# The first pass of a graph network: aggregation placed inside the other stream's layer, and stores issued by ScalarE

## Chip, cores, metric

One NeuronCore of a Trainium2 chip. The metric is the device time of one execution in microseconds (us), the slowest core's; with one core it is that core's. Three runs of the kernel before gave 2013.59, 2016.44 and 2018.27 us, median 2016.44.

## What is computed

Four layers over x of 128 graphs x 64 nodes x 256 features with one 64 x 64 adjacency matrix; each layer adds a graph network's output to x and normalises. Layer 0, whose first half is the subject here, is

```python
A_norm = A + eye(n)
deg = sum(A_norm, axis=0) + sum(A_norm, axis=1) - diagonal(A_norm)
A_hat = A_norm * rsqrt(deg)[:, None] * rsqrt(deg)[None, :]
agg = einsum('nm,bmd->bnd', A_hat, x)
h = relu(batchnorm(agg.reshape(-1, d) @ W1.T + b1, g1, be1))     # 256 -> 512
out = batchnorm(h @ W2.T + b2, g2, be2)                          # 512 -> 256
x = layernorm(x + out)
```

Layer 1 is a Chebyshev convolution with the largest eigenvalue of the matrix, attention and a feed-forward part; layer 2 two graph convolutions and LSTMs over windows; layer 3 a graph attention. The batch norms take their mean and variance over all 8192 tokens, so layer 0 needs three passes over the tokens.

## The kernel before

All weights stay in SBUF, each split into a high and a low f16 part (`w_hi`, `w_lo`), so that a product takes three f16 matmuls (L454 to L456: high x high, high x low, low x high). Tokens come in 16 tiles of 512 (8 graphs); tile (r, s) belongs to round r of 8 and stream s of 2. Each stream has its own buffers and its own 4 PSUM banks `ps[s]` of 512 f32 columns.

Three blocks follow one another. Block 1 (L562 to L879), the subject, computes for every tile h = agg @ W1.T + b1, its statistics, and stores h to DRAM (`h_scratch`). Block 2 (L895 to L1088) reads h back, applies the batch norm and relu and multiplies by W2. Block 3 is the rest of the network, some 1770 us, whose order of work per engine is written out by hand in `ORDER`.

Block 1, per engine. The engines run their own lists in order and meet only at semaphores.

- TensorE (PE), L747 to L768. `aggregate(s, n)` (L724): 64 matmuls of 64 x 64 in f32 (`quarters`, L468) into banks 0 and 1 of `ps[s]`, after waiting for the tile of x and for the four reads of the stream's banks. `hidden(s, n, ms)` (L734): 6 matmuls of 128 x 512 for each of four output parts m; the banks are 2, 3, 0, 1 for stream 0 and 2, 0, 1, 2 for stream 1. `square(j, which)` (L717): the squarings of a 64 x 64 matrix for the eigenvalue, one or two small f32 matmuls that depend on DVE. A round is aggregate(0), aggregate(1), then for each stream hidden m 0 and 1, square, hidden m 2 and 3, square.
- ScalarE (ACT), L699 to L708. `agg_high` (L678) casts the aggregate to f16 (L680); `unit_high` (L672) casts one unit of 1408 weight columns (L675); `hid_bias` (L682) moves the four parts from PSUM to `hid[s]` with the bias (L687), after waiting until the store of the stream's last tile has landed and its statistics are taken. A round is agg_high(0), agg_high(1), then for each stream unit_high and hid_bias of four.
- VectorE (DVE), L843 to L860. `agg_low` (L830) takes the low part of the aggregate (L832); `unit_low` (L777) that of the weights (L780); `hid_stat` (L835) the statistics of `hid` of the round before (L838); `square` (L818) the normalisation, copy and trace (L821 to L827).
- SyncE (SP), L591 to L609, issues all DMAs: `load_x` (L586), 512 KB, after the tile's aggregate; `load_unit` (L582), 704 KB, after DVE has used the unit before; `store` (L577), 1024 KB, after the tile's four biases. A round is load_x(0), load_x(1), then for each stream load_unit and store.

The weights are read in 16 units in the course of the block, two a round; W1 is in unit 0.

Of the kernel before, what the change touches and what calls it, by code (L numbers as in the profile page):

```python
# [8 lines left out]
ALU = mybir.AluOpType  # L9
# [3 lines left out]
P = 128  # L13
# [7 lines left out]
HT = HID // P  # L21
# [354 lines left out]
def build(nc, x, adj, adj_t, wpack, w3t, cols, rows, out):  # L376
    ctx = ExitStack()
    with ctx:
# [120 lines left out]
        with ExitStack() as pctx:  # L499
# [48 lines left out]
            spare = ps[1][:, BANKS - 1, :]  # L548
            SQ, TR, LAM, WA = spare[0:NODES, 0:NODES], spare[:, 64:65], spare[:, 66:68], spare[:, 72:72 + 2 * KT]

            GCN, SUMS = (ps[0][:, BANKS - 1, j * P:(j + 1) * P] for j in range(2))
            def aggregated(s):
                return ps[s][:, 0:2, :].rearrange('p c (j n) -> p j c n', n=NODES)

# [7 lines left out]
            @block.sync  # L562
            def _(sp):
                sp.wait_ge(zeroed, 2)
                for b in range(2):
                    d = slice(b * NODES, (b + 1) * NODES)
                    sp.dma_start(a_bd[d, d], adj).then_inc(adj_in, 16)
                    sp.dma_start(at_bd[d, d], adj_t).then_inc(adj_in, 16)
                for s in range(STREAMS):
                    sp.dma_start(xa[s][:, :, :], x_tiles[1, s]).then_inc(x_in[s], 16)  # L570
                sp.dma_start(stage[0], wpack[:, 0:UNIT]).then_inc(w_in[0], 16)
                sp.dma_start(col[:, :], cols).then_inc(vec_in, 16)
                sp.dma_start(stage[1], wpack[:, UNIT:2 * UNIT]).then_inc(w_in[1], 16)
                sp.dma_start(w3t_sb[:, 0:KT, :], w3t).then_inc(vec_in, 16)
                sp.dma_start(row[:, :, :], rows.partition_broadcast(P)).then_inc(row_in, 16)

                def store(s, n):  # L577
                    sp.wait_ge(hid_out[s], n * HT + 1)
                    sp.dma_start(h_tiles[bass.ds(n, 1), s].rearrange("o p m n -> (o p) m n"), hid[s])\
                        .then_inc(hid_stored[s], 16)  # L580

                def load_unit(r, b):  # L582
                    sp.wait_ge(unit_lo, r * STAGES + b - (STAGES - 1))
                    sp.dma_start(stage[b], wpack[:, bass.ds(r * (STAGES * UNIT) + b * UNIT, UNIT)]).then_inc(w_in[b], 16)

                def load_x(s, r, tile):  # L586
                    sp.wait_ge(agg_ps[s], r)
                    sp.dma_start(xa[s][:, :, :], x_tiles[bass.ds(tile, 1), s].rearrange("o p b d -> (o p) b d"))\
                        .then_inc(x_in[s], 16)

                for b in range(STAGES):  # L591
                    load_unit(1, b)
                with sp.Fori(1, ROUNDS - 1) as r:
                    for s in range(STREAMS):
                        load_x(s, r, r + 1)
                    for s in range(STREAMS):
                        load_unit(r + 1, s)
                        store(s, r)

                for s in range(STREAMS):  # L600
                    load_x(s, ROUNDS - 1, 0)
                for s in range(STREAMS):
                    store(s, ROUNDS - 1)
                for s in range(STREAMS):
                    sp.wait_ge(unit_lo, UNITS)
                    sp.wait_ge(hid_stored[s], 17)
                    sp.dma_start(first_hid[s], h_tiles[1, s]).then_inc(h_in[1][s], 16)
                for s in range(STREAMS):
                    sp.wait_ge(hid_stored[s], 16 * (ROUNDS - 1) + 1)  # L609
# [56 lines left out]
            @block.scalar  # L666
            def _(act):
                act.wait_ge(ident_ok, 5)
                for s in range(STREAMS):
                    nc.scalar.activation(small[:, 40 + s:41 + s], ident[:, 0:1], ACT.Copy).then_inc(hid_out[s], 1)  # L670

                def unit_high(r, b):  # L672

                    act.wait_ge(w_in[b], r * 16 + 16)
                    nc.scalar.activation(w_hi[:, bass.ds(r * (STAGES * UNIT) + b * UNIT, UNIT)], stage[b], ACT.Copy,  # L675
                                         scale=WSCALE).then_inc(unit_hi, 1)

                def agg_high(s, n):  # L678
                    act.wait_ge(agg_ps[s], n)
                    nc.scalar.copy(by_batch(hl_a[s][:, 0, :, :]), aggregated(s)).then_inc(agg_hi[s], 1)  # L680

                def hid_bias(s, n):  # L682
                    act.wait_ge(hid_stored[s], n * 16 - 15)
                    act.wait_ge(hid_stats[s], n)
                    for m in range(HT):
                        act.wait_ge(hid_ps[s], n * HT - (HT - 1 - m))
                        nc.scalar.activation(hid[s][:, m, :], ps[s][:, hid_bank[s][m], :], ACT.Identity,  # L687
                                             bias=vec("b1", m), scale=UNSCALE).then_inc(hid_out[s], 1)

                unit_high(0, 0)  # L690
                act.wait_ge(step, 7)
                for j in range(HALF):
                    part = slice(j * P, (j + 1) * P)
                    nc.scalar.copy(sums[0:1, part], SUMS[0:1, :])
                    nc.scalar.copy(sums[64:65, part], SUMS[64:65, :])
                    nc.scalar.copy(sums[32:33, part], SUMS[32:33, :]).then_inc(rows_ok, 1)
                unit_high(0, 1)
                act.wait_ge(vec_in, 32)
                with act.Fori(0, ROUNDS - 1) as r:  # L699
                    for s in range(STREAMS):  # L700
                        agg_high(s, r + 1)
                    for s in range(STREAMS):
                        unit_high(r + 1, s)
                        hid_bias(s, r + 1)
                for s in range(STREAMS):
                    agg_high(s, ROUNDS)
                for s in range(STREAMS):
                    hid_bias(s, ROUNDS)  # L708

            @block.tensor  # L710
            def _(pe):
# [5 lines left out]
                def square(j, which):  # L717
                    pe.wait_ge(sq_ready, j * 3 + 2 + which)
                    pe.sem_inc(begun, 1)
                    if which == 0:  # L720
                        nc.tensor.matmul(TR, ones[0:NODES, :], tr_part, start=True, stop=True)
                    nc.tensor.matmul(SQ, powr, powr, start=True, stop=True).then_inc(sq_ps, 1)
# [21 lines left out]
                        mm.then_inc(hid_ps[s], 1)  # L744

                pe.wait_ge(step, 7)
                with pe.Fori(0, ROUNDS - 1) as r:  # L747
                    for s in range(STREAMS):
                        aggregate(s, r + 1)
                    for s in range(STREAMS):  # L750
                        hidden(s, r + 1, range(HT // 2))
                        square(r * STREAMS + s, 0)
                        hidden(s, r + 1, range(HT // 2, HT))
                        square(r * STREAMS + s, 1)
                for s in range(STREAMS):
                    aggregate(s, ROUNDS)
                hidden(0, ROUNDS, range(HT))
                pe.wait_ge(vec_in, 32)
                pe.wait_ge(sq_ready, 3 * (SQUARINGS // 2) + 3)
                nc.tensor.matmul(LAM, ones[0:NODES, :], lam_part, start=True, stop=True)  # L760
# [10 lines left out]
            def _(dve):  # L771
# [5 lines left out]
                def unit_low(r, b):  # L777
# [2 lines left out]
                    nc.vector.scalar_tensor_tensor(w_lo[:, part], stage[b], WSCALE, w_hi[:, part], ALU.mult,  # L780
                                                   ALU.subtract).then_inc(unit_lo, 1)

                dve.wait_ge(adj_in, 64)
                dve.wait_ge(ident_ok, 5)

# [12 lines left out]
                nc.vector.tensor_scalar(scaled, junk_full, dinv, None, ALU.mult).then_inc(step, 1)  # L798
                dve.wait_ge(gcn_ps, 1)
                nc.vector.tensor_scalar(gcn_t[:, :], GCN, dinv, None, ALU.mult).then_inc(step, 1)  # L800
                unit_low(0, 0)

                nc.vector.tensor_tensor(sym, a_bd[0:NODES, 0:NODES], at_bd[0:NODES, 0:NODES], ALU.add).then_inc(step, 1)
# [23 lines left out]
                        nc.vector.tensor_tensor_reduce(junk, powr, powr, 1.0, 0.0, ALU.mult, ALU.add, tr_part)\  # L827
                            .then_inc(sq_ready, 1)

                def agg_low(s, n):  # L830
                    dve.wait_ge(agg_hi[s], n)
                    nc.vector.tensor_tensor(by_batch(hl_a[s][:, 1, :, :]), aggregated(s), by_batch(hl_a[s][:, 0, :, :]), ALU.subtract)\  # L832
                        .then_inc(agg_lo[s], 1)

                def hid_stat(s, r, ms):  # L835
                    for m in ms:
                        dve.wait_ge(hid_out[s], r * HT + m + 2)
# [4 lines left out]

                with dve.Fori(0, ROUNDS - 1) as r:  # L843
                    for s in range(STREAMS):
                        agg_low(s, r + 1)
                    for s in range(STREAMS):
                        unit_low(r + 1, s)
                        hid_stat(s, r, range(HT // 2))
                        square(r * STREAMS + s, 0)
                        hid_stat(s, r, range(HT // 2, HT))  # L850
                        square(r * STREAMS + s, 1)
                for s in range(STREAMS):
                    agg_low(s, ROUNDS)
                dve.wait_ge(sq_ready, 3 * (SQUARINGS // 2) + 2)
                nc.vector.tensor_tensor_reduce(junk, sym, powr, 1.0, 0.0, ALU.mult, ALU.add, lam_part[:, 0:1])\
                    .then_inc(pow_ok, 1)
                dve.wait_ge(pow_ok, 2)
                nc.vector.tensor_tensor_reduce(junk, ident[0:NODES, 0:NODES], powr, 1.0, 0.0, ALU.mult, ALU.add,
                                               lam_part[:, 1:2]).then_inc(sq_ready, 1)
                hid_stat(0, ROUNDS - 1, range(HT))  # L860


                dve.wait_ge(hid_stats[0], ROUNDS + 1)
# [1281 lines left out]
```

## Time and profile before

| | us |
|---|---|
| median of three runs | 2016.44 |
| the profiled execution | 2013.94 |
| its span, first to last instruction | 2012.1 |
| block 1, until PE's last hidden product ends | about 143.5 |
| waits of PE for DVE L832 in block 1 | 16.0 |

The busy times of the page are sums over the whole span. A timeline row gives start, duration, engine, line and operation, with the idle time of the engine before it in brackets. PEld is PE's loading of weights, which overlaps its matmuls; a matmul of 512 columns has a duration of 0.38 us there, though they start 0.22 us apart, since they are pipelined. "DMA share" is the mean busy share of 16 DMA engines, as the tool gives it; it goes slightly above 1 in short windows.

### The profile page before, as it was taken

Reading aid. Unit: us, or ns where it says so; the run is one execution under the profiler, and the core shown is the slowest. Engines: PE = TensorE matmul, PEld = TensorE weight load, DVE = VectorE, ACT = ScalarE, POOL = GpSimd, SP = SyncE. Lnnn points to the kernel's source line nnn. Section 1 sums busy time; section 2 is a strip of 40 time slices with the busy share of each in tenths; the row PEclk is TensorE's granted clock in tenths of the full one; section 3 lists DMA queues with packets and bytes.
Section 4 is the critical chain, followed back from the end, with each engine's and each line's share of the span. In section 5 each row is a group of like instructions: output and inputs, shape, how many; then the busy total and the mean of one; then the engine's idle time right before and its main releaser. Section 6 shows DMA issues by size and latency. Waiting matters only on the chain.

```text
span 2012.1 us, 85711 instructions
## 1 busy us (share of the span) xinstructions
PE 1944.8 (97%) x37031; PEld 1730.6 (86%) x37031; DVE 1718.2 (85%) x4795; ACT 1443.6 (72%) x4475; POOL 187.8 (9%) x258
## 2 busy tenths in 40 slices
PE   6899989999999999999999999999999999999997
PEld 3444469999999999999999999999999999999996
DVE  6779897888888988898889888898889888988866
ACT  5657537777777777767777777777777777777777
POOL 2000010110101010101001110101010101111000
PEclk9999999999999999999999999999999999999999
DMA  7857400000100001000100010000000010000000
GB/s 281 290 196 253 175 2 23 14 13 4 44 3 24 3 3 45 13 13 3 44 14 13 4 44 4 23 3 14 34 13 13 3 45 13 13 3 13 3 3 23
DMA packets 36822, 87.79 MB, mean 44 GB/s; under 512 B 2416, under 2 KB 26992, under 8 KB 32752
## 3 DMA queue, kind: packets, MB, share of 16 engines
q1 hardware_dynamic: 36464, 82.56, 11.8%
q8 instruction: 280, 4.59, 1.0%
q14 instruction: 78, 0.64, 0.1%
HBM read 52.15 MB, written 30.41 MB: 41 GB/s over the span
## 4 chain that ended last, share of the span: by engine, by line
PE 78%; ACT 5%; DVE 4%; issue 1%; POOL 0%; ACTq 0%; DVEq 0%
PE ps L1539 18%; PE ps L1568 11%; PE ps L1548 9%; PE ps L1353 8%; PE ps L1387 7%; PE ps L1575 5%; PE ps L1363 4%; PE ps L1395 3%; PE ps L468 2%; PE ps L1330 2%; ACT pool_mem L1726 2%; PE ps L1320 1%; PE ps L1627 1%; PE ps L1595 1%; PE ps L1441 1%; DVE stats L1849 1%
## 5 line engine op out<-in xcount | busy, mean ns | idle before, releaser
L1726 ACT ACTIVATE pool_mem<-ps,lstm_b 128x64 f32<-128x64 f32 (+2 forms) x2496 | 606.2, 364 | 147.0 <-PE ps L1575 102.6
L1539 PE MATMUL ps<-hl_a,w_hi 128*128 128x64 f16 (+1 forms) x3584 | 361.3, 205 | 1.8 <-DVE hl_a L2005 0.9
L1539 PE MATMUL ps<-hl_a,w_lo 128*128 128x64 f16 (+1 forms) x3584 | 360.8, 205 | 0.0
L1818 POOL TENSOR_TENSOR rstd<-mv,nhalf 128x2 f32<-128x2 f32 x224 | 174.1, 779 | 1592.3 <-DVE mv L1853 1592.3
L1539 PEld LDWEIGHTS ps<-hl_a,w_hi 128*128 128x128 f16 x3584 | 284.4, 97 | 6.3 <-DVE hl_a L2005 1.2
L1539 PEld LDWEIGHTS ps<-hl_a,w_lo 128*128 128x128 f16 x3584 | 283.0, 97 | 2.8
L1568 PE MATMUL ps<-pool_mem,w_hi 128*128 128x64 f16 (+2 forms) x3072 | 273.6, 200 | 0.0
L1568 PE MATMUL ps<-pool_mem,w_lo 128*128 128x64 f16 (+2 forms) x3072 | 273.5, 199 | 0.0
L1548 PE MATMUL ps<-hl_a,w_hi 128*128 128x64 f16 (+1 forms) x3584 | 233.5, 205 | 0.2 <-issue 0.2
L1568 PEld LDWEIGHTS ps<-pool_mem,w_hi 128*128 128x128 f16 x3072 | 228.9, 98 | 2.9
L1568 PEld LDWEIGHTS ps<-pool_mem,w_lo 128*128 128x128 f16 x3072 | 227.7, 98 | 0.7
L1548 PEld LDWEIGHTS ps<-hl_a,w_hi 128*128 128x128 f16 x3584 | 177.4, 97 | 0.9 <-issue 0.3
L1575 PE MATMUL ps<-pool_mem,w_hi 128*128 128x64 f16 (+2 forms) x3072 | 175.4, 200 | 0.0
L1849 DVE BATCH_NORM_STATS2 stats<-t 128x6 f32<-128x256 f32 x448 | 168.2, 417 | 5.5
L1735 ACT ACTIVATE pool_mem<-pool_mem 128x256 f32<-128x256 f32 (+2 forms) x352 | 129.2, 379 | 53.2 <-DVE pool_mem L1989 28.7
L1983 DVE SCALAR_TENSOR_TENSOR pool_mem<-pool_mem 128x256 f32<-128x256 f32 (+2 forms) x352 | 118.8, 340 | 38.7 <-ACT pool_mem L1726 36.4
L1387 PE MATMUL ps<-hl_b,w_hi 128*128 128x256 f16 x640 | 150.3, 273 | 0.4 <-DVE hl_b L1898 0.2
L1387 PE MATMUL ps<-hl_b,w_lo 128*128 128x256 f16 x640 | 150.2, 273 | 0.0
L2002 DVE SCALAR_TENSOR_TENSOR pool_mem<-pool_mem 128x256 f32<-128x256 f32 (+2 forms) x352 | 123.9, 356 | 28.9 <-ACT pool_mem L1735 27.8
L1575 PEld LDWEIGHTS ps<-pool_mem,w_hi 128*128 128x128 f16 x3072 | 135.9, 98 | 0.0
L1539 PE MATMUL ps<-hl_b,w_hi 128*128 128x84 f16 x1408 | 130.4, 201 | 0.5
L1539 PE MATMUL ps<-hl_b,w_lo 128*128 128x84 f16 x1408 | 130.5, 200 | 0.0
(253 smaller groups left out, 4768.8 us busy)
## 6 DMA issues: line engine op xcount, KB each, us to landing
xa<-in_x SPq DMA_DIRECT2D x32, 512.0 KB, 5.4
h_scratch<-pool_mem SPq DMA_DIRECT2D x14, 1024.0 KB, 4.4
pool_mem<-h_scratch SPq DMA_DIRECT2D x14, 1024.0 KB, 6.8
pool_mem<-in_wpack SPq DMA_DIRECT2D x16, 704.0 KB, 4.2
out<-xb SPq DMA_DIRECT2D x16, 512.0 KB, 3.4
o_scratch<-act_in SPq DMA_DIRECT2D x14, 512.0 KB, 3.2
act_in<-o_scratch SPq DMA_DIRECT2D x14, 512.0 KB, 5.0
row<-in_rows SPq DMA_DIRECT2D x1, 1408.0 KB, 11.7
```

The costliest lines, as they stand in the source:

```text
L1353: nc.tensor.matmul(tok(s, bank)[:, b, :], hi, w[part], start=k == 0 and b == 0 and part == 0, stop=False, skip_group_check=True)
L1387: nc.tensor.matmul(out[:, j, :], w[part], hi[:, k, :], start=j == 0 and k == 0 and part == 0, stop=False, skip_group_check=True)
L1539: nc.tensor.matmul(o, wk[part], toks[0][:, k], start=(g, m) == gms[0] and k == 0 and part == 0, stop=False, skip_group_check=True)
L1548: mm = nc.tensor.matmul(o, weight(f"wih{p}", k, (g * KT + m) * P, P)[0], toks[1][:, k], start=False, stop=step == 0 and (g, m) == gms[-1] ...
L1568: nc.tensor.matmul(gate_place(s, h, g, m, w), wk[part], hi[:, k * w:(k + 1) * w], start=False, stop=False, skip_group_check=True)
L1575: mm = nc.tensor.matmul(gate_place(s, h, g, m, w), weight(f"whh{p}", k, (g * KT + m) * P, P)[0], lo[:, k * w:(k + 1) * w], start=False, st ...
L1726: op = nc.scalar.activation(gates[s][h][:, g, m * w:(m + 1) * w], gate_place(s, h, g, m, w), ACT.Tanh, bias=lstm_b[:, bias:bias + 1], scal ...
L1735: nc.scalar.activation(cell_t[s][h][:, 0:KT * w], cell_c[s][h][:, 0:KT * w], ACT.Tanh, scale=0.5)\
L1818: nc.gpsimd.tensor_tensor(rstd[s][:, blocks(h)], mv[s][:, blocks(h), 1], nhalf[:, 0:HALF], ALU.pow)\
L1849: nc.vector.bn_stats(stats[s][:, b, 0:6], t[s][:, b, :]).then_inc(ln_step.of(s, h), 1)
L1983: nc.vector.scalar_tensor_tensor(cc if first else g[GATE_I], g[GATE_I], 1.0, g[GATE_G], ALU.add, ALU.mult).then_inc(cell_dve.of(s, h), 1)
L2002: nc.vector.scalar_tensor_tensor(to, o, 1.0, th, ALU.add, ALU.mult).then_inc(cell_dve.of(s, h), 1)
```

## The change

In block 1 the aggregate of the other stream goes between the two halves of a stream's `hidden` on PE, and the cast, the subtraction and the loads of ACT, DVE and SP are put in the matching order; aggregate(0, 1) is done ahead of the loop. The stores of h leave SP's list and are issued by ACT. `SUMS` moves to another bank. Cut to what matters:

```diff
-            GCN, SUMS = (ps[0][:, BANKS - 1, j * P:(j + 1) * P] for j in range(2))
+            GCN = ps[0][:, BANKS - 1, 0:P]
+            SUMS = ps[1][:, 2, 0:P]
 SP
+                load_x(0, 1, 2)
                 for b in range(STAGES):
                     load_unit(1, b)
-                with sp.Fori(1, ROUNDS - 1) as r:
-                    for s in range(STREAMS):
-                        load_x(s, r, r + 1)
+                load_x(1, 1, 2)
+                with sp.Fori(1, ROUNDS - 2) as r:
                     for s in range(STREAMS):
                         load_unit(r + 1, s)
-                        store(s, r)
-
+                        load_x(s, r + 1, r + 2)
                 for s in range(STREAMS):
+                    load_unit(ROUNDS - 1, s)
                     load_x(s, ROUNDS - 1, 0)
-                for s in range(STREAMS):
-                    store(s, ROUNDS - 1)
 ACT
-                def hid_bias(s, n):
-                    act.wait_ge(hid_stored[s], n * 16 - 15)
-                    act.wait_ge(hid_stats[s], n)
-                    for m in range(HT):
+                def hid_bias(s, n, ms):
+                    if 0 in ms:
+                        act.wait_ge(hid_stored[s], n * 16 - 15)
+                        act.wait_ge(hid_stats[s], n)
+                    for m in ms:
...
+                def store(s, n):
+                    act.wait_ge(hid_out[s], n * HT + 1)
+                    nc.scalar.dma_start(h_tiles[bass.ds(n, 1), s].rearrange("o p m n -> (o p) m n"), hid[s])\
+                        .then_inc(hid_stored[s], 16)
+
+                agg_high(0, 1)
                 unit_high(0, 0)
...
                 with act.Fori(0, ROUNDS - 1) as r:
-                    for s in range(STREAMS):
-                        agg_high(s, r + 1)
-                    for s in range(STREAMS):
-                        unit_high(r + 1, s)
-                        hid_bias(s, r + 1)
-                for s in range(STREAMS):
-                    agg_high(s, ROUNDS)
-                for s in range(STREAMS):
-                    hid_bias(s, ROUNDS)
+                    hid_bias(0, r + 1, range(HT // 2))
+                    agg_high(1, r + 1)
+                    unit_high(r + 1, 0)
+                    hid_bias(0, r + 1, range(HT // 2, HT))
+                    store(0, r + 1)
+                    hid_bias(1, r + 1, range(HT // 2))
+                    agg_high(0, r + 2)
+                    unit_high(r + 1, 1)
+                    hid_bias(1, r + 1, range(HT // 2, HT))
+                    store(1, r + 1)
+                hid_bias(0, ROUNDS, range(HT // 2))
+                agg_high(1, ROUNDS)
+                hid_bias(0, ROUNDS, range(HT // 2, HT))
+                hid_bias(1, ROUNDS, range(HT))
 PE
                 pe.wait_ge(step, 7)
+                aggregate(0, 1)
+                pe.wait_ge(unit_lo, 1)
                 with pe.Fori(0, ROUNDS - 1) as r:
-                    for s in range(STREAMS):
-                        aggregate(s, r + 1)
                     for s in range(STREAMS):
                         hidden(s, r + 1, range(HT // 2))
                         square(r * STREAMS + s, 0)
+                        aggregate(1 - s, r + 1 + s)
                         hidden(s, r + 1, range(HT // 2, HT))
                         square(r * STREAMS + s, 1)
-                for s in range(STREAMS):
-                    aggregate(s, ROUNDS)
-                hidden(0, ROUNDS, range(HT))
+                hidden(0, ROUNDS, range(HT // 2))
+                aggregate(1, ROUNDS)
+                hidden(0, ROUNDS, range(HT // 2, HT))
 DVE
                 nc.vector.tensor_scalar(gcn_t[:, :], GCN, dinv, None, ALU.mult).then_inc(step, 1)
+                agg_low(0, 1)
                 unit_low(0, 0)
...
                 with dve.Fori(0, ROUNDS - 1) as r:
                     for s in range(STREAMS):
-                        agg_low(s, r + 1)
-                    for s in range(STREAMS):
+                        hid_stat(s, r, range(1))
+                        square(r * STREAMS + s, 0)
+                        hid_stat(s, r, range(1, HT // 2))
+                        agg_low(1 - s, r + 1 + s)
                         unit_low(r + 1, s)
-                        hid_stat(s, r, range(HT // 2))
-                        square(r * STREAMS + s, 0)
+                        square(r * STREAMS + s, 1)
                         hid_stat(s, r, range(HT // 2, HT))
-                        square(r * STREAMS + s, 1)
-                for s in range(STREAMS):
-                    agg_low(s, ROUNDS)
...
-                hid_stat(0, ROUNDS - 1, range(HT))
+                hid_stat(0, ROUNDS - 1, range(HT // 2))
+                agg_low(1, ROUNDS)
+                hid_stat(0, ROUNDS - 1, range(HT // 2, HT))
```

## Rows read from the trace of the kernel before

**Rows 1.** The page's first part: busy time, share and instructions of each engine.
```profile
PE 1944.8 (97%) x37031; PEld 1730.6 (86%) x37031; DVE 1718.2 (85%) x4795; ACT 1443.6 (72%) x4475; POOL 187.8 (9%) x258
```

**Rows 2.** Waits, 0 to 145 us: engine, line, releaser, total us, times, longest.
```profile
PE ps L454 <- DVE hl_a L832: 16.0, 8, 5.6
ACT w_hi L675 <- DMA pool_mem<-in_wpack: 11.0, 2, 8.1
```

**Rows 3.** Timeline of one round, 60 to 80 us, around the aggregates.
```profile
63.95 1.99 PEld L468 LDWEIGHTS ps<-gcn_t,xa 64*64 64x64 f32 x128
...
65.23 1.95 ACT L680 CAST hl_a<-ps 128x1024 f16<-128x1024 f32 x2 [0.55 <-PE ps L468]
65.43 0.20 DVE L825 COPY x<-ps 64x64 f32<-64x64 f32 x1
...
65.81 0.08 DVE L827 DVE_READ_ACCUMULATOR2_ANT setup<- 64x1 f32 x1
66.27 2.35 DVE L832 TENSOR_TENSOR hl_a<-ps,hl_a 128x1024 f16<-128x1024 f32 x2 [0.39 <-ACT hl_a L680]
...
67.55 0.39 PE L454 MATMUL ps<-hl_a,w_hi 128*128 128x512 f16 x1 [1.48 <-DVE hl_a L832]
...
69.06 0.69 ACT L687 ACTIVATE pool_mem<-ps,col 128x512 f32<-128x512 f32 x1 [0.61 <-PE ps L456]
```

**Rows 4.** Timeline, 110 to 150 us: the same start in the last round.
```profile
130.89 0.39 PE L454 MATMUL ps<-hl_a,w_hi 128*128 128x512 f16 x1 [1.48 <-DVE hl_a L832]
```

**Rows 5.** Windows: length, busy us and instructions of each engine, granted clock, DMA share, GB/s.
```profile
63.90:79.80 15.90, 14.42 (x190) 7.63 (x190) 12.28 (x23) 9.87 (x12) 0.00 (x0) 1.00 0.83 289
...
70.00:72.00 2.00, 2.00 (x12) 1.08 (x11) 1.61 (x5) 0.69 (x1) 0.00 (x0) 1.00 1.16 390
```

**Rows 6.** Timeline, stream 1's half of that round.
```profile
73.76 0.39 PE L454 MATMUL ps<-hl_a,w_hi 128*128 128x512 f16 x1
...
76.45 0.29 PEld L721 LDWEIGHTS ps<-setup,x 64*128 64x128 f32 x2 [0.42 <-issue]
...
76.56 0.69 ACT L687 ACTIVATE pool_mem<-ps,col 128x512 f32<-128x512 f32 x1 [0.42 <-PE ps L456]
76.76 0.19 PEld L722 LDWEIGHTS ps<-x 64*64 64x64 f32 x2
...
77.02 0.39 PE L454 MATMUL ps<-hl_a,w_hi 128*128 128x512 f16 x1
```

**Rows 7.** Timeline, 57 to 62 us: a weight unit on ACT and DVE.
```profile
58.37 1.37 ACT L675 ACTIVATE w_hi<-pool_mem 128x1408 f32 x1
...
59.89 1.63 DVE L780 SCALAR_TENSOR_TENSOR w_lo<-pool_mem,w_hi 128x1408 f32 x1 [0.21 <-ACT w_hi L675]
```

**Rows 8.** Timeline, 0 to 34 us: the start of block 1.
```profile
9.29 3.53 PEld L468 LDWEIGHTS ps<-gcn_t,xa 64*64 64x64 f32 x128 [1.10 <-issue]
...
11.20 1.38 ACT L675 ACTIVATE w_hi<-pool_mem 128x1408 f16<-128x1408 f32 x1 [8.13 <-DMA pool_mem<-in_wpack]
...
14.26 3.43 SPq L584 DMA_DIRECT2D pool_mem<-in_wpack  x2
...
18.65 0.61 PE L454 MATMUL ps<-hl_a,w_hi 128*128 128x512 f16 x1 [5.64 <-DVE hl_a L832]
...
20.27 1.38 ACT L675 ACTIVATE w_hi<-pool_mem 128x1408 f32 x1 [2.84 <-DMA pool_mem<-in_wpack]
...
21.19 0.54 PE L454 MATMUL ps<-hl_a,w_hi 128*128 128x512 f16 x1
```

**Rows 9.** SP's wait, 15 to 145 us; issues (ns min/median/max) of x and stores; stores' landing.
```profile
SPq L579 <- ACT pool_mem L687: 49.0, 14, 7.2
...
L588 SPq DMA_DIRECT2D xa<-in_x x14: 383/396/1257, 18.0 to 113.7; - x14
...
L579 SPq DMA_DIRECT2D h_scratch<-pool_mem x14: 355/362/382, 27.0 to 128.0; - x14
...
DMA to landing us min/median/max: 3.9/4.4/5.1
```

More of the change, by code:

```diff
@@ L575, in _ @@
                 sp.dma_start(row[:, :, :], rows.partition_broadcast(P)).then_inc(row_in, 16)
[L577 to L580, printed above, removed]
                 def load_unit(r, b):
@@ L781, in unit_low, with agg_low @@
                                                    ALU.subtract).then_inc(unit_lo, 1)
+                def agg_low(s, n):
+                    dve.wait_ge(agg_hi[s], n)
+                    nc.vector.tensor_tensor(by_batch(hl_a[s][:, 1, :, :]), aggregated(s), by_batch(hl_a[s][:, 0, :, :]), ALU.subtract)\
+                        .then_inc(agg_lo[s], 1)
                 dve.wait_ge(adj_in, 64)
@@ L828, in square @@
                             .then_inc(sq_ready, 1)
[L830 to L833, printed above, removed]
                 def hid_stat(s, r, ms):
```

## The prediction

> **What bounds the kernel now.** The page comes first: TensorE (PE) is busy for 97% of the span [rows 1], so time comes off almost only where PE stands still or does other work. The change touches the first block alone, so next come its waits [rows 2]. The reader is to see one large wait of PE: 8 times, once per round, it stood before a `hidden` for DVE's `agg_low` (L832), 16.0 us in all, 5.6 the first time. Third, a round at close hand [rows 3]: both aggregates run back to back (128 weight loads, 1.99 us from 63.95), ScalarE (ACT) casts both (from 65.23), DVE subtracts (from 66.27), and PE starts `hidden(0)` at 67.55, having stood still for 1.48 us. Fourth, the same hidden start 4 rounds later is at 130.89 [rows 4], so a round is (130.89 - 67.55)/4 = 15.83 us. In such a round DVE is busy for 12.28 us, ACT for 9.87, and the DMA engines 0.83 of the time at 289 GB/s [rows 5]. Three resources thus stand not far behind PE.
>
> **Part 1, aggregation inside the other stream's layer, steady rounds.** No matmul, cast or subtraction is added or removed; they move. Half a round, in PE's own time from its first hidden matmul, is read from stream 1's half, which no aggregate cuts today [rows 6]: start 73.76, the first squaring's loads at 76.45 (2.69), the second pair of products at 77.02 (3.26). The other half's 67.55 to 73.76 is 6.21. An aggregate costs 1.99/2 = 1.0 us of loads [rows 3]. So a half becomes 6.2 + 1.0 = 7.2 and a round 14.4, if nothing waits: 15.83 - 14.4 = **1.4 saved in each of 7 rounds, 9.9 us**. The switch back from small f32 loads to a hidden matmul inside a layer is not in the trace; after a squaring it takes 0.07 (0.19 of loads from 76.76, then 77.02), after an aggregate it may take from nothing to 0.28 (from the end of a first aggregate's loads, 63.95 + 1.0, to its cast at 65.23, the row nearest to a drained array). I take the 0.07, small f32 loads too, and keep 0.2 x 14 = 3 us for the range.
>
> Does nothing wait? The chain that has to fit in the half, each link from rows:
> - PE's aggregate of the other stream begins at about 3.1. Today ACT starts the first cast 1.28 after the first aggregate begins (63.95, 65.23), so ACT casts at 4.4 to 4.5.
> - ACT has done both biases of this half by then (the first starts 1.51 after the hidden start, 69.06 against 67.55, the second at 2.80, each 0.69 [rows 3, 6]), so it is free at 3.5: slack 1.0.
> - DVE starts 1.04 after the cast's start (65.23, 66.27), at 5.5, and PE can begin 1.28 after that (66.27, 67.55), at 6.8. PE needs it at 7.2. **Slack 0.4 us: the thinnest link.**
> - ACT then does the weight unit (1.37) and two biases (0.69 each), until about 8.1, then the store. DVE does the subtraction (1.2), the unit (1.63, started 0.15 after ACT's) and the squaring's copy and trace (0.46, 65.43 to 65.89), which ends at 9.0 [rows 3, 7]; PE wants that for its next squaring at 7.2 + 2.7 = 9.9. Slack 0.9. DVE's work, 12.28, is 85% of 14.4; it has the last two statistics done at about 10.2, in time for its next subtraction at 12.7.
> - An aggregate also waits until all four banks of its stream are read; the last bias ends at 8.1, the aggregate of that stream comes at 10.3.
>
> **Part 1, the start.** Today the aggregates begin at 9.29, take 3.53 of loads for 128, and PE waits for ACT's unit (from 11.20), DVE's unit and then both casts and subtractions until 18.65 [rows 8]. After: one aggregate is through at about 11.3; ACT casts it (0.97) before unit 0, which has landed by 11.20, and so ends unit 0 at 13.7; DVE subtracts till 13.6 and ends the unit's low half near 15.5; PE waits for just that. So hidden begins at 15.5 and not at 18.65: **3.1 us**. PE's first six matmuls start 0.42 apart (18.65 to 21.19), twice the later 0.22, and take 0.61 and not 0.38: the lower of its two levels, 1.2 and not 2.4 GHz, though the granted clock of the stretch reads 1.00; before them it had stood for 5.64 us [rows 8]. I leave that cost, 6 x 0.2 = 1.2 us, as it is, and keep as much again for the range. The first refill of a unit is asked for at 15.5 instead of 14.26; it landed 6.0 us after issue (20.27), so 21.5, and ACT wants it at 22.3. `SUMS` only changes its bank: nothing.
>
> **Part 1, the end.** The last hidden(0) now holds one aggregate: +1.0 us against the two that stood before it, already counted in 9.9 as out of the round. The LAM and WA products stay. Net of part 1: 9.9 + 3.1 - 1.0 = **12.0 us**.
>
> **Part 2, stores on ACT's queue.** Fourteen stores of 1024 KB leave SP, where they stood for 49.0 us in all before their condition came [rows 9]; the loads behind them in SP's order were never late: the only two waits for a load are ACT's, 11.0 us, at the start [rows 2]. So the move in itself gives nothing. It costs ACT the issue. No row shows ACT issue a DMA; SP needed 0.36 for a store, and up to 1.26 for a load close behind other transfers [rows 9]. I take 0.36 (one a half, the last long landed). From 8.1 in a half ACT has until 11.7 (its next cast) for the issue and two biases (1.3): 2.2 us are free, so either end costs nothing. The wait placed before the store is for ACT's own last bias.
> The store must land before the same stream's next bias, `hid_stored`: issued at about 8.4, wanted at 14.4 + 1.5 = 15.9, so 7.5 us. Stores landed after 3.9 to 5.1, median 4.4 [rows 9]. Now stores share the engines with the unit (704 KB) that SP asks for at the same moment; both are 1.77 MB, and windows with the engines busiest move 390 GB/s [rows 5]: 4.5 us, and the 1.7 that a store takes beyond its bytes at that rate (4.4 - 2.7) make 6.2. It fits. Both ends: 4.4, as now, and 6.2; I take the latter. DMA per round stays 4.6 MB, 11.8 us at 390 GB/s, under 14.4.
> On the rule's side: the Trainium skill (DMA: Bandwidth & Descriptors, "Issuing engines are not separate DMA queues") says transfers issued by several engines run on the same 16 DMA engines and interleave, which saves only issue time. It speaks against a gain from part 2, as the waits above do, and for the second rival below; by the same page's queue section an engine takes turns between queues packet by packet, so that a store would get half the rate while a load is queued. The sum by it is the same.
>
> **Sum.** 12.0 off. The profiled execution, on which it is made, took 2013.94 us (span 2012.1), 2.5 below the median of the three runs shown, 2016.44. The blocks behind only start earlier. Predicted median: 2016.44 - 12.0 = **2004.4 us**, profiled about 2001.9.
>
> **Rivals.**
> 1. *`agg_low` comes late.* The slack is 0.4 us and rests on sums of seven links. If ACT or DVE is 0.4 to 0.9 later than drawn (a dearer ACT issue, a bias behind the unit), PE waits up to 0.5 in each of 14 halves: 7 us back, **2011**. For it: the thin slack. Against it: ACT and DVE both have 1.0 us free just ahead of their link. Chance 0.13.
> 2. *The store lands too late* (the other side). At L684 the bias waits for `hid_stored`; the cast stands behind it on ACT, DVE behind the cast, PE behind DVE. The place has 7.5 us, plus 1.7 until two late biases push the cast, plus 0.4: it decides from a landing of 9.6, and eats the gain where the halves lose 12.0/14 = 0.86 each, at 10.5. At 12 us of landing: 2.4 x 14 = 34 lost, 12 won, **2038**. For it: engines at 0.83 that would go to 0.91. Against it: my 6.2, and the 5.1 of the slowest store now. Chance 0.05.
> 3. *The order gives less than drawn* (the aggregate does not pack behind a squaring, and the low clock level lasts longer at the start: 3 + 1.2, or a loss as large again): 4.5 to 10 off the gain, **2009 to 2014**. That is also where the change doesn't do what it says. Chance 0.12.
> The forecast itself, 9.5 to 14.5 off: chance 0.70.
>
> **From cases to numbers.** A measurement of this kernel tells a difference of about 0.2% (4 us) from none. The forecast, rival 1 and two thirds of rival 3 lie beyond 4 us: with some allowance for a fault in the drawing faster 0.86, within 0.2% 0.08, slower 0.06. Range: low 2000.0 (14.5 off and 2 of spread between runs), high 2011.5 (rival 1 whole).
>
> **What would show it.** Right: PE's wait for DVE L832 falls from 16.0 us in 8 to one of about 4 at the start; hidden(0) starts 14.4 apart; the second block starts about 12 us earlier; ACT gets 14 issues near 0.4 us. Wrong: PE waits for L832 each half (rival 1); ACT L687 waits for the DMA of h_scratch (rival 2); rounds above 14.7 with no wait (rival 3); any move of time behind the first block.

## The result and the profile after

The changed kernel took **2002.66 us** in the median of six runs (2000.76 to 2003.57), the kernel before 2015.21 in six on the same chip (2013.59 to 2018.27): a ratio of 0.9935, 95% interval 0.9923 to 0.9948, or 12.55 us less. The forecast was 2004.4 us, 12.0 less than the 2016.44 of three runs, and about 2001.9 for the profiled execution, which took 2002.39 us with a span of 2000.6.

The waits of the first 135 us, engine, line, releaser, total us, times and longest, are the answer to [rows 2]. In the new kernel `hidden` is still L454, ACT's cast of the aggregate is L674, its unit L669, its biases L682, its store L687; DVE's `agg_low` is L792, its `unit_low` L787. A "slow product" below is a matmul of 512 columns at the lower level of the clock: 0.43 us from its start to the next one's, and not 0.22.

```profile
ACT pool_mem L682 <- PE ps L456: 29.7, 36, 2.9
ACT hl_a L674 <- PE ps L468: 20.4, 16, 7.9
DVE hl_a L792 <- ACT hl_a L674: 16.6, 16, 3.2
...
PE ps L454 <- DVE w_lo L787: 4.2, 1, 4.2
```

PE's wait for `agg_low`, 16.0 us in 8 times before, is gone; left is one at the start, for the unit's low half. ACT waits for PE and not for a transfer.

The timeline of the start, to hold against [rows 8]: one aggregate, its cast ahead of the unit, and PE at `hidden` at 15.15 instead of 18.65.

```profile
8.93 1.99 PE L468 MATMUL ps<-gcn_t,xa 64*64 64x64 f32 x64 [0.54 <-DVE gcn_t L812]
10.97 1.01 ACT L674 CAST hl_a<-ps 128x1024 f16<-128x1024 f32 x1 [7.90 <-PE ps L468]
11.88 1.38 ACT L669 ACTIVATE w_hi<-pool_mem 128x1408 f16<-128x1408 f32 x1
12.02 1.23 DVE L792 TENSOR_TENSOR hl_a<-ps,hl_a 128x1024 f16<-128x1024 f32 x1 [3.24 <-ACT hl_a L674]
...
13.29 1.62 DVE L787 SCALAR_TENSOR_TENSOR w_lo<-pool_mem,w_hi 128x1408 f16<-128x1408 f32 x1
...
15.15 0.61 PE L454 MATMUL ps<-hl_a,w_hi 128*128 128x512 f16 x1 [4.24 <-DVE w_lo L787]
15.55 0.63 PE L455 MATMUL ps<-hl_a,w_hi 128*128 128x512 f16 x1
```

The timeline of a steady half, which began at 67.60 (half a round before 74.74), to hold against [rows 3, 6]:

```profile
70.67 1.05 PEld L468 LDWEIGHTS ps<-gcn_t,xa 64*64 64x64 f32 x61
...
71.79 0.39 PE L454 MATMUL ps<-hl_a,w_hi 128*128 128x512 f16 x1
...
71.95 1.01 ACT L674 CAST hl_a<-ps 128x1024 f16<-128x1024 f32 x1 [0.86 <-PE ps L468]
...
72.99 1.23 DVE L792 TENSOR_TENSOR hl_a<-ps,hl_a 128x1024 f16<-128x1024 f32 x1 [0.90 <-ACT hl_a L674]
...
74.14 1.26 ACT L682 ACTIVATE pool_mem<-ps,col 128x512 f32<-128x512 f32 x2
...
74.74 0.39 PE L454 MATMUL ps<-hl_a,w_hi 128*128 128x512 f16 x1
...
75.55 0.34 ACTq L687 DMA_DIRECT2D h_scratch<-pool_mem  x1
...
76.18 0.34 SPq L580 DMA_DIRECT2D pool_mem<-in_wpack  x1
...
76.39 0.69 ACT L682 ACTIVATE pool_mem<-ps,col 128x512 f32<-128x512 f32 x1 [0.99 <-PE ps L456]
```

PE never stands. `agg_low` starts at 72.99; before, PE followed it by 1.28 [rows 3], so it could start at 74.27 and does at 74.74: 0.47 us to spare. A whole round by windows (columns as in [rows 5]):

```profile
74.74:89.03 14.29, 14.29 (x190) 7.58 (x188) 11.95 (x23) 9.64 (x14) 0.00 (x0) 1.00 0.95 325
```

PE is busy for 14.29 us of 14.29; DVE, ACT and the DMA engines have come nearer (DMA share 0.95 instead of 0.83). At the end of block 1 both kernels have 19 filler products (L474, the helper `keep_clock`, whose results nobody reads), then 13 more at the start of block 2, before its first real product (L454). The row of the first filler stands where the last hidden product has made way; its start is called the end of block 1 from here on. First the changed kernel:

```profile
131.39 4.26 PE L474 MATMUL ps<-w_hi 128*128 128x512 f16 x19
135.95 2.97 PE L474 MATMUL ps<-w_hi 128*128 128x512 f16 x13 [0.30 <-PEq L499]
139.61 0.39 PE L454 MATMUL ps<-hl_a,w_hi 128*128 128x512 f16 x1 [0.69 <-DVE hl_a L1005]
```

Then the kernel before:

```profile
143.46 4.26 PE L474 MATMUL ps<-w_hi 128*128 128x512 f16 x19
...
151.68 0.39 PE L454 MATMUL ps<-hl_a,w_hi 128*128 128x512 f16 x1 [0.69 <-DVE hl_a L997]
```

Block 1 ends 12.07 us earlier, and block 2's first real product starts 12.07 earlier. From the first of the 13 fillers to the end of the span it takes 1864.65 us (from 135.95), before 1864.07 (from 148.03). That untouched rest took 1863.4 to 1867.1 us in the profiled executions below, so single times are compared at the end of block 1, where fractions of a us can be read.

### The profile page after: what moved, and what is told of

Read it like the earlier page. It is cut to its first block, busy times and chain, and to the rows that moved or that the text cites. A ratio compares the mean times of both kernels' runs of the same rounds, so it can differ in the third digit from the quotient of the medians.

```text
span 2000.6 us, 85730 instructions
## 1 busy us (share of the span) xinstructions
PE 1945.0 (97%) x37031; PEld 1729.7 (86%) x37031; DVE 1717.0 (86%) x4795; ACT 1444.4 (72%) x4475; POOL 187.7 (9%) x258
## 4 chain that ended last, share of the span: by engine, by line
PE 78%; ACT 5%; DVE 4%; issue 1%; POOL 0%; ACTq 0%; DVEq 0%
PE ps L1547 19%; PE ps L1576 11%; PE ps L1556 9%; PE ps L1361 8%; PE ps L1395 7%; PE ps L1583 6%; PE ps L1371 4%; PE ps L1403 3%; PE ps L468 2%; PE ps L1338 2%; ACT pool_mem L1734 2%; PE ps L1328 1%; PE ps L1635 1%; PE ps L1449 1%; PE ps L1603 1%; DVE stats L1857 1%
```

## Experiments

The edits are shown shortened; `...` marks what is left out.

**One part at a time.** e1 keeps the new order and leaves the stores on SP; e2 keeps the old order and moves only the stores.

```diff
 e1: the changed kernel, SP's loop (and the same at its end)
                 for s in range(STREAMS):
+                    store(s, r)
                     load_unit(r + 1, s)
                     load_x(s, r + 1, r + 2)
 e2: the kernel before, ACT's loop (SP's stores taken out)
                     unit_high(r + 1, s)
                     hid_bias(s, r + 1)
+                    store(s, r + 1)
```

> Only the order is changed; SP goes on issuing the stores, each ahead of the unit and the tile of x that come after it in time. Mine: the stores' queue gives nothing, so this takes what the whole change takes: rounds of 14.3 us, PE's last hidden product of block 1 ending near 131.4 as there, a median 12 us below the kernel before. Rival (the second queue carries part of the gain, since SP's waits stand ahead of the loads): at least 2 us of the 12 are missing, rounds above 14.4, ACT or PE waiting for a DMA.

> Only the stores move to ACT; the order is that of before. Mine: rounds stay at 15.83 us, PE's last hidden product ends near 143.5, median within 0.1% of the kernel before. Rival (the queue itself gives something): block 1 ends at least 1 us earlier; rival (ACT's issue costs): at least 1 us later, 14 issues of 0.4 being 5 us if they stood on the path.

e1: median 2001.87 us in 4 runs, ratio 0.993 (0.9914 to 0.9947); end of block 1 at 131.38. The order alone (of all four engines' lists, with the start that is done ahead of the loop) gives the whole gain. The issues stand at the same times as in the changed kernel, each row from e1's timeline:

```profile
75.55 0.36 SPq L589 DMA_DIRECT2D h_scratch<-pool_mem  x1
76.18 0.33 SPq L580 DMA_DIRECT2D pool_mem<-in_wpack  x1
```

Its stores land after 4.1/4.8/5.2 us (shortest, median, longest) and its units after 5.4/6.0/6.3. On two queues, in the changed kernel, they are 4.0/4.7/5.0 and 5.2/5.8/6.3. The second queue changes neither by more than 0.2. The Trainium skill (DMA: Bandwidth & Descriptors, "Issuing engines are not separate DMA queues") says that transfers of several issuers run on the same engines; the two runs agree.

e2: median 2020.06 us in 10 runs, ratio 1.0023 (1.0013 to 1.0032): slower, where my pricing of part 2 expected nothing. Block 1 ends at 148.29, 4.83 later than before: 0.69 a round. The timeline of e2 in a round (L679 bias, L684 store, L667 unit, L672 cast):

```profile
59.51 0.69 ACT L679 ACTIVATE pool_mem<-ps,col 128x512 f32<-128x512 f32 x1 [0.61 <-PE ps L456]
...
60.36 0.34 ACTq L684 DMA_DIRECT2D h_scratch<-pool_mem  x1
60.83 1.38 ACT L667 ACTIVATE w_hi<-pool_mem 128x1408 f32 x1 [0.63 <-ACT pool_mem L679]
...
62.12 1.25 ACT L679 ACTIVATE pool_mem<-ps,col 128x512 f32<-128x512 f32 x2
...
65.73 0.69 ACT L679 ACTIVATE pool_mem<-ps,col 128x512 f32<-128x512 f32 x1 [0.61 <-PE ps L456]
66.39 1.99 PEld L468 LDWEIGHTS ps<-gcn_t,xa 64*64 64x64 f32 x128 [0.53 <-issue]
```

The unit follows the bias's start by 1.32 us. In the kernel before it followed by 0.59 (58.37 [rows 7] against the bias at 57.78). The store's place costs ACT 0.73: it waits for its own last bias to be complete, then issues for 0.34. In the old order the unit stands between two streams' biases, so stream 1's first two biases come late (62.12, both behind one another), the last at 65.73, and the aggregates, which want the banks, begin behind it. Only that store, one of the two of a round, is on that way: the other is issued at 66.57, while PE has the aggregates in hand, and ACT still waits 1.23 for PE ahead of its next cast at 67.64. In the new order the same 0.73 falls into the 0.99 us in which ACT waits for PE (76.39, above).

**How thin is the slack of `agg_low`?** A delay ahead of each cast, by small copies on ACT.

```diff
 ACT, agg_high, behind its waits
+                    for j in range(3):          # e5: range(9)
+                        nc.scalar.activation(small[:, 48 + j:49 + j], ident[:, 0:1], ACT.Copy)
```

> The changed kernel with three one-column copies on ACT ahead of each cast, a delay of about 0.35 us, under the slack of 0.47 that I read. Mine: rounds stay at 14.29 and no wait of PE for the subtraction appears in them. Rival (there is no slack, the copies go onto the path): rounds of 14.9 to 15.0, block 1 ends 5 us later.

> The changed kernel with nine one-column copies on ACT ahead of each cast of an aggregate, which should delay it by about 0.9 us (two such copies took 0.29). Mine: the slack between DVE's subtraction and PE's next hidden is 0.47 us, so PE waits about 0.45 us for DVE before each of 14 halves: round 15.2, block 1 ends 6 us later, PE's wait for the subtraction's line 6 us in all. Rival (the slack is larger, because something else sets PE's start): less than 2 us later.

e4's cast comes 0.30 later: no wait of PE in the rounds, round 14.29, end of block 1 at 131.69, and 2001.82 us in one run. e5's comes 0.86 later. From its waits, and its timeline (L676 cast, L794 `agg_low`):

```profile
PE ps L454 <- DVE w_lo L789: 5.1, 1, 5.1
PE ps L454 <- DVE hl_a L794: 4.1, 14, 0.3
```

```profile
74.23 0.95 ACT L675 ACTIVATE small<-ident 128x1 f32<-128x1 f32 x9 [0.86 <-PE ps L468]
75.09 0.99 ACT L676 CAST hl_a<-ps 128x1024 f16<-128x1024 f32 x1
...
76.11 1.22 DVE L794 TENSOR_TENSOR hl_a<-ps,hl_a 128x1024 f16<-128x1024 f32 x1 [1.26 <-ACT hl_a L676]
...
77.39 0.39 PE L454 MATMUL ps<-hl_a,w_hi 128*128 128x512 f16 x1 [0.29 <-DVE hl_a L794]
```

Half a round grows by 0.36 us (7.145 to 7.51). Block 1 ends 6.50 later: 14 x 0.36 = 5.0, 0.7 at the start (15.86), 0.9 back from a shorter slow stretch there (7 products and not 12), and 1.7 from a fall of the clock near the end that e3 has too (below). The time is 2007.8 us in one run. The slack is 0.86 - 0.36 = 0.50 by this, 0.47 by the timeline and 0.4 in the prediction: rival 1 was a real edge, half a microsecond away.

**Are the transfers near their edge?** 256 KB more with each load of x.

```diff
 SP, load_x
+                    sp.wait_ge(extra_in[s], r * 16 - 15)
+                    sp.dma_start(xb[0][:, s * 2:s * 2 + 2, :], x_tiles[...][:, 0:2, :]).then_inc(extra_in[s], 16)
```

> The changed kernel with a further load of 256 KB behind each load of x from round 2 on, into a buffer that this block does not use: 2.56 MB and not 2.29 a half, at 390 GB/s 6.6 us of DMA in a half of 7.14. Mine: the DMA engines go from 0.93 to near 1.0 of the time, landings grow to 6 to 7 us, and the rounds stay at 14.3, since stores have 7.5 us. Rival (the stores' landing is already near its limit): ACT's bias waits for the store's DMA and rounds grow past 14.5.

One run of 2003.3 us; the windows of two rounds:

```profile
31.90:46.19 14.29, 14.29 (x189) 7.58 (x188) 11.96 (x23) 9.64 (x12) 0.00 (x0) 1.00 1.02 366
74.70:88.99 14.29, 14.29 (x190) 7.58 (x188) 11.96 (x23) 9.64 (x12) 0.00 (x0) 1.00 1.03 364
```

Stores land after 4.9/6.1/7.0 us and nobody waits for them (ACT waits once, 0.4 us, for a weight unit); the round stays 14.29 with the DMA engines' share above 1. Block 1 ends at 130.58, 0.81 earlier than in the changed kernel, with 8 slow products at the start and not 12; an execution of the unaltered kernel shows the same (e10 below). Rival 2 (a store later than 9.6) was far: here a share near 1 said nothing by itself; the landing against the time allowed did.

**The start.** e3 puts the first cast and subtraction behind the units, where the kernel before had them; the aggregation stays in the new order.

```diff
 ACT
-                agg_high(0, 1)
                 unit_high(0, 0)
...
+                agg_high(0, 1)
 DVE: agg_low(0, 1) likewise, from ahead of unit_low(0, 0) to just ahead of the loop
```

> The changed kernel, but the first cast and subtraction come after both weight units, as before; the rounds are untouched. The first hidden product then starts near 18.5 us and not at 15.15. Mine of the start (3.1 us come from this, the cost of the low clock level moves with the start): block 1 ends later by 3.3 us if the level rises a fixed amount of work after the hidden starts (12 matmuls at 0.42 as in the changed kernel). Rival: the level rises near 20 to 21 us of the span whenever hidden starts, so that only 5 or 6 matmuls are slow, as in the kernel before, and block 1 ends only about 2.1 us later.

`hidden` starts at 18.62 [7.58 behind DVE L792], 3.47 later, near what I expected (18.5), but block 1 ends at 136.77, 5.38 later (2006.44 us in one run). 0.2 lies in the first half, and 1.7 in the last round, where the clock fell a second time. Its timeline and windows:

```profile
128.10 1.95 PE L771 MATMUL ps<-col,t 128*128 128x1 f32 x16
129.91 0.59 PE L454 MATMUL ps<-hl_a,w_hi 128*128 128x512 f16 x1
...
133.28 0.42 PE L456 MATMUL ps<-hl_a,w_lo 128*128 128x512 f16 x1
133.53 0.38 PE L454 MATMUL ps<-hl_a,w_hi 128*128 128x512 f16 x1
```

```profile
130.00:133.00 3.00, 3.00 (x9) 1.08 (x8) 0.00 (x0) 0.25 (x1) 0.00 (x0) 0.50 0.44 180
```

The granted clock of that stretch reads 0.50, the lower level, after 16 products of one column each. The same 16 stand in the changed kernel at 124.41 with no such fall behind them, so this 1.7 is not time that PE waits for the moved cast. What is left for the cast's place is 3.47 + 0.2, near the 3.3 that I expected. The 12 slow products (18.62 to 23.7) speak against the rival, by which the level rises at a fixed time near 20 to 21; that their number is fixed by the work done is not shown either, as e10 gives 8 of them in an unaltered kernel.

**What the lower level costs at the start.** The changed kernel has 12 slow products there (15.15 to 20.2), where the kernel before had 7 (18.65 to 21.6, the last of them in part; the prediction counted the six steps between them). Products on zeros fill PE's idle time: e8 11 of them ahead of the first aggregate, e7 those and 14 behind it.

```diff
 PE
+                pe.wait_ge(warm_ok, 1)
+                for j in range(11):
+                    nc.tensor.matmul(ps[0][:, 2, :], hl_b[0][:, 0, 0, 0:P], hl_b[0][:, 0, 0, :], start=True, stop=True)
...
                 aggregate(0, 1)
+                for j in range(14):             # e7 alone
+                    nc.tensor.matmul(...)
                 pe.wait_ge(unit_lo, 1)
```

> The changed kernel with 11 matmuls of 512 columns on zeros from about 2.5 us, while PE has nothing, and 14 more after the first aggregate. If PE's work before is what raises the clock level: the first aggregate takes 1.0 and not 1.83 us of loads, the 12 slow hidden matmuls (0.42 apart) become 0.22 apart, and block 1 ends 2.5 to 3.3 us earlier. Rival (the level rises at a fixed time near 20 us, whatever PE does): the aggregate and 12 matmuls stay slow, nothing is gained, and the 25 added matmuls at 0.42 delay the first hidden by 1 to 3 us.

> Only the first 11 of those matmuls. If work before raises the level and a stand of 4 us lowers it again: the aggregate is fast (1.0 us), the hidden matmuls are slow again, block 1 ends 0 to 1 us earlier. If the stand does not lower it: as e7_warm_both. Rival (fixed time): no change.

e7: no slow product in `hidden`, block 1 ends at 129.32, 2.07 earlier than in the changed kernel; median 1999.56 us in 4 runs, ratio 0.9926 (0.9909 to 0.9943). e8: about 10 slow ones, end at 130.56, 2000.73 us in one run. In e7 the level was up before the first row of zeros ended (its 11 products took 3.83 us; at 0.43 each they would take 4.7) and was down again behind the 1.95 us in which PE stood; its windows:

```profile
8.00:10.00 2.00, 1.46 (x49) 1.27 (x50) 0.35 (x1) 0.00 (x0) 1.44 (x4) 0.50 1.08 400
```

so the first aggregate took 1.99 us there too. In e11 below, the same kernel, PE stood for only 0.91 us at that place (the zeros took 4.76), and the aggregate took 1.16. In e8 it was 1.46 and 1.95.

**More at the start, and the same kernel again.** e9 also casts and subtracts unit 0 in two pieces, the columns of the first product first; e10 is the changed kernel unaltered.

```diff
 ACT (DVE and PE's wait in the same way, 13 and 14 products on zeros)
-                unit_high(0, 0)
+                nc.scalar.activation(w_hi[:, 0:W1], stage[0][:, 0:W1], ACT.Copy, scale=WSCALE).then_inc(w1_hi, 1)
+                nc.scalar.activation(w_hi[:, W1:UNIT], stage[0][:, W1:UNIT], ACT.Copy, scale=WSCALE).then_inc(unit_hi, 1)
```

> The changed kernel with 13 matmuls on zeros ahead of the first aggregate, 14 behind it, and the first unit of w_in cast and subtracted in two pieces, the 1024 columns that the first hidden product reads first. If the start of PE's work is set by that unit's cast and subtraction (11.88 to 15.12 in the changed kernel), two of three parts of it are taken off the way for the hidden product (the first piece is a third of the columns), the first hidden product starts near 14.2 instead of 15.15 and, with the level of the clock already up, PE's last hidden product ends near 128.5 instead of 131.39: some 3 us earlier, of which the warm-up alone gave 2.1. The median is then some 3 us below that of the changed kernel run on the same chip. Rivals: the second warm-up row now ends after the first piece is there, so that the start stays near 15.0 and the gain at 2.1; or the up to 3 us by which the untouched rest of the program differed from run to run hide it, and the medians are within 1 us.

> The changed kernel itself, unaltered, timed beside the run before it on the same chip. Every theory expects 2002 to 2003 us, 12 to 13 us below the kernel before, PE's last hidden product at 131.4, and at the first hidden product some 12 matmuls at the lower level of the clock; if the number of these differs from run to run whatever the kernel, it may be as few as 6, and the end 1 us earlier.

e9: median 2001.54 us (5 runs), e10: 2001.77 (5 runs), 0.9927 (0.9913 to 0.994): no difference. `hidden` did start at 13.68, better than the expected 14.2, but block 1 ends at 130.84. e9's timeline (L673 a unit, L740 and L859 of a squaring) and windows:

```profile
21.59 1.38 ACT L673 ACTIVATE w_hi<-pool_mem 128x1408 f32 x1 [2.55 <-DMA pool_mem<-in_wpack]
...
25.28 0.35 PE L740 MATMUL ps<-setup,x 64*128 64x1 f32 x2 [1.70 <-DVE setup L859]
...
27.09 0.61 PE L454 MATMUL ps<-hl_a,w_hi 128*128 128x512 f16 x1
27.50 0.63 PE L455 MATMUL ps<-hl_a,w_hi 128*128 128x512 f16 x1
```

```profile
10.00:22.00 12.00, 11.21 (x114) 5.46 (x113) 8.78 (x16) 7.91 (x14) 5.40 (x9) 1.00 1.03 402
...
26.00:30.00 4.00, 4.00 (x65) 2.10 (x57) 3.52 (x7) 2.48 (x4) 0.00 (x0) 0.57 0.99 319
```

The next unit lands at 21.6, though it was asked for at 13.94. In e7 and e11 it was asked for at 14.78 and 14.27 and is there at 21.70 and 21.77, so asking sooner doesn't bring it sooner; that full DMA engines are the reason (share 1.03 at 402 GB/s since 10) fits, but no run takes their load away. ACT waits for the unit, DVE's squaring stands behind that unit, PE waits 1.70 for the squaring, and behind that wait the clock is down: six more products at 0.43 instead of 0.22. A wait of that length doesn't always have this behind it: in e11 PE stood for 1.70 ahead of its first `hidden` (14.48), and none of its products was slow. What the start gave was taken back 11 us later.

e10's profile holds 8 slow products in `hidden` and ends block 1 at 130.42, the first profile of the same kernel 12 and 131.39. PE's rows in e10, with the step from one level to the other:

```profile
15.02 0.60 PE L454 MATMUL ps<-hl_a,w_hi 128*128 128x512 f16 x1 [4.24 <-DVE w_lo L787]
...
17.98 0.54 PE L455 MATMUL ps<-hl_a,w_hi 128*128 128x512 f16 x1
18.35 0.38 PE L456 MATMUL ps<-hl_a,w_lo 128*128 128x512 f16 x1
```

**Does e7 beat the changed kernel?** Both again, on one chip.

> The kernel of e7_warm_both once more, beside the changed kernel on the same chip, to tell whether it beats the changed kernel. If the warm-up takes off the matmuls at the lower level each time, PE's last hidden product ends near 129.3 and the median is 1 to 2 us below that of e12_after_third (1 where the changed kernel happens to have 8 such matmuls, 2 where it has 12). Rival: what the level costs differs from run to run with the warm-up too, or the 3 us by which the rest of the program differs hide it, and the medians are within 0.5 us.

> The changed kernel unaltered, to be compared with e11_warm_again on the same chip. 2001.5 to 2003 us, 12 to 14 us below the kernel before, PE's last hidden product at 130.4 (8 slow matmuls, as in e10_after_again) to 131.4 (12 of them, as in the first profile).

e11 2002.10 us (1999.54 to 2004.26, 5 runs), e12 2003.86 (2001.17 to 2006.78, 6 runs); ratios 0.9928 (0.9915 to 0.9942) and 0.9937 (0.9924 to 0.9949). Block 1 ends at 129.41 and 131.33 (12 slow products). In block 1 the warm-up gives 1.9 to 2.1 us against the executions with 12 slow products, and 1.0 to 1.1 against e10, which had 8; in the median of whole runs 1.8 lie between them, which the overlapping intervals don't prove. PE waits for the same squaring, in stream 1's half of the first round, in e7 (0.49 us, from 24.90), e11 (1.07, from 24.39) and e9 (1.70, from 23.58), and always until 25.3 to 25.5. That is the next bound: at the higher level this squaring comes 9.9 us after the first `hidden` (14.99 to 24.90), so a `hidden` that starts before 25.4 - 9.9 = 15.5 gains nothing. What e7 and e11 gained is the level, not their earlier start: e11's `hidden` starts 0.51 before e7's and its block 1 ends 0.09 later.

## Why the prediction was right, point by point

| step | predicted | measured |
|---|---|---|
| first `hidden` | 15.5 | 15.15 |
| half a round | 7.2 | 7.145 |
| aggregate inside a layer | 1.0 (1.07 with the switch back) | 0.93 |
| cast, `agg_low`, PE free to start, from the half's start | 4.4 to 4.5, 5.5, 6.8 | 4.35, 5.39, 6.67 |
| slack of `agg_low` | 0.4 | 0.47 to 0.50 |
| ACT done; squaring's trace done | 8.1; 9.0 | 7.80; 8.80 |
| ACT's issue | 0.36 | 0.34 |
| store's landing | 6.2 | 4.7 |
| slow products at the start | 6 by their steps (7 products) | 12 (8 in e10, 12 in e12) |

- **The rounds.** From the first `hidden` to that of the last round it was 112.24 us (18.65 to 130.89), and is 102.46 (15.15 to 117.61): 9.78 less. The rounds themselves gave 7 x (15.83 - 14.29) = 10.8, more than 9.9, because the aggregate's first loads run between those of the squaring (61 of 64 behind it). The switch back takes 0.07 (loads until 71.72, `hidden` at 71.79), just what the prediction read. It said that it took this 0.07, but its 7.2 is 6.21 + 1.0 without it; with it the rounds would have come to 8.9. The longer slow stretch took 1.0 back: the first round was 2.43 longer than a steady one (31.87 - 15.15 - 14.29), before 1.40 (35.88 - 18.65 - 15.83). That is the one term of part 1 that was mis-sized ("I leave that cost as it is"). That it and the error of the rounds came to nearly nothing together is luck.
- **The start** gave 3.50, against 3.1; **the end** cost 1.21 (13.78 us of last round instead of 12.57), against 1.0. 9.78 + 3.50 - 1.21 = 12.07, which is what block 1 shows. The 12.55 between the medians has an interval of 10.5 to 15.5 and agrees with it. Of the 1.7 us between the forecast 2004.4 and 2002.66, 1.2 come from the kernel before, whose median was 2016.44 in three runs and 2015.21 in six.
- **Part 2** "costs nothing and gives nothing": true in the new order (e1 against the changed kernel, 131.38 and 131.39). The statement that either end of the issue's price costs nothing held because of the 0.99 us of ACT's idle time, which e2 lacks. The price itself was incomplete: beside the issue of 0.34 there is the wait for ACT's own last bias, 0.73 together, which the prediction named and did not price. In e2 that made a kernel slower than before.
- **Landing.** I added the transfers up and took the unit's share as the store's. In the runs the store, issued 0.6 us ahead, hardly pays (4.4 to 4.7); the unit does (4.1 before, 5.8 after), which nobody waits for. Half the rate for the store, as the prediction worked it out for two queues, was not seen.
- **Rivals.** 1: the edge is where it was drawn, but 0.5 us away. 2: e6 at a landing of 6.1, up to 7.0, shows no loss. 3: rounds were shorter than drawn, the low level was longer, by 1.0, within the allowance of 1.2.

## What to carry to other kernels

If the pipe that sets the time stands for a producer at a known place in each round, look for work of the *other* stream to put ahead of it, and add up every link from that work to the next need; here seven links read from rows of the trace gave the slack to 0.1 us. Price an issue moved to a busy engine with the wait for that engine's own last result, and find what stands behind it: the same store was free in one order and cost 4.8 us in the other. Before shortening a start further, look at what the earlier start needs sooner: here the next weights, which came no sooner for being asked for sooner.

## What was not expected of the hardware

- The number of products at the lower level (1.2 GHz, 0.43 us apart) behind the same start differed from one execution of the same kernel to the next: 12, 8 and 12 (until 20.2, 18.4 and 20.1), which is 1 us of block 1 (131.39, 130.42, 131.33). So the kernel alone doesn't set it; what does stays open.
- The granted clock of a window does not show that first stretch: at 15 to 18 us of the changed kernel it reads 1.00, while the products are 0.43 apart. A fall after the level had once been up does show (0.50 in e3 and e7, 0.57 in e9).

```profile
15.00:18.00 3.00, 2.85 (x7) 1.04 (x8) 2.85 (x8) 1.23 (x2) 1.42 (x5) 1.00 1.04 388
```

- The 16 products of one column were followed by a fall of the clock, nine slow products (the last in part) and 1.7 us, in e3 and e5, and by none in the other twelve profiled executions. In e5 two products at the higher level stood between. In these two the 16 came later than in the changed kernel (128.10 and 129.22 against 124.41), but lateness alone doesn't make the fall: in the kernel before and in e2 they came later still (136.48 and 141.30), with none behind them. The cause stays open.
